# A token-mixing and channel-mixing layer over eight sequences: the low-rank products in other PSUM banks, the chunk products copied by two engines, and a new order of the steps

## The reference, cut to what matters

```python
xn  = ln(x);  sx = shift(xn) - xn
xxx = tanh((xn + sx * maa_x) @ maa_w1)          # 5 low-rank parts of 32
x5  = xn + sx * (maa_stack + xxx @ maa_w2)      # 5 mixes of 512
w   = exp(-exp(time_decay + tanh(x5[1] @ decay_w1) @ decay_w2))
r, k, v = x5[3] @ Wr.T, x5[0] @ Wk.T, x5[2] @ Wv.T
g   = silu(x5[4] @ Wg.T)
# per head, token by token:  out = r . (u * k v + s);  s = k v + w * s
x   = x + group_norm(out) * g @ Wo.T
xn2 = ln(x);  xk, xr = mixes of xn2 and its shift
x   = x + sigmoid(xr @ ffn_Wr.T) * (square(relu(xk @ ffn_Wk.T)) @ ffn_Wv.T)
```

## Time and profile before

| | us |
|---|---|
| median of 3 timed runs (lowest, highest) | 770.8 (770.7, 773.09) |
| the profiled execution, its own time | 774.99 |
| its span | 773.2 |
| TensorE busy in the span | 699.0 |
| VectorE busy | 526.0 |
| GpSimd busy | 391.6 |
| ScalarE busy | 326.6 |

### The profile page before, as it was taken

How to read it: one execution, slowest core, us unless ns; L and a number is a source line. 1 busy time by engine, 2 the same in 40 slices (tenths; PEclk the granted TensorE clock), 3 DMA queues, 4 the chain that set the end, 5 groups by cost and what they waited for, 6 DMA issues and landing times.

```text
span 773.2 us, 17240 instructions
## 1 busy us (share of the span) xinstructions
PE 699.0 (90%) x7260; PEld 478.7 (62%) x7260; DVE 526.0 (68%) x771; ACT 326.6 (42%) x639; POOL 391.6 (51%) x223
## 2 busy tenths in 40 slices
PE   2798889998999899998899989998999979995777
PEld 2586576657774676656675676755876557753453
DVE  3628846896768847796668965886767944679541
ACT  1053463328531583328441394316642274324311
POOL 1054953556566565566356665557456634463000
PEclk9999599999999999999999999999999979999689
DMA  6900000002000200002000020002000010000000
GB/s 205 392 2 8 29 2 1 1 2 89 3 1 1 86 7 1 3 1 90 3 1 1 18 73 2 0 2 90 3 1 1 5 59 3 27 2 1 3 27 27
DMA packets 13130, 24.57 MB, mean 32 GB/s; under 512 B 3840, under 2 KB 5632, under 8 KB 12032
## 3 DMA queue, kind: packets, MB, share of 16 engines
q1 hardware_dynamic: 13056, 23.47, 8.8%
HBM read 18.35 MB, written 4.19 MB: 29 GB/s over the span
## 4 chain that ended last, share of the span: by engine, by line
PE 82%; DVE 7%; issue 5%; ACT 4%; SPq 1%; DMA 1%; POOL 0%; POOLq 0%; ACTq 0%; DVEq 0%
PE FB L588 28%; PE FA L874 8%; PE BAB L856 7%; PE FB L596 7%; PE FA L897 6%; PE BAB L762 5%; PE FA L667 4%; PE BAB L833 3%; PE BAB L799 2%; PE FB L632 2%; PE BAB L579 2%; ACT wide L1040 2%; PE BAB L813 1%; DVE half L1377 1%; PE FB L628 1%
## 5 line engine op out<-in xcount | busy, mean ns | idle before, releaser
L503 POOL TENSOR_TENSOR pp<-rT,kT 128x2048 f32<-128x2048 f32 (+1 forms) x32 | 108.9, 3413 | 58.5 <-DVE rT L1281 58.5
L465 POOL TENSOR_TENSOR mixes<-mixes 128x1024 f32<-128x1024 f32 x30 | 76.6, 2552 | 116.1 <-ACT mixes L1010 116.1
L467 POOL TENSOR_TENSOR mixes<-mixes,xnT 128x1024 f32<-128x1024 f32 x30 | 74.4, 2478 | 2.4
L588 PE MATMUL FB<-mixes,wk_s 128*128 128x256 f32 x256 | 63.0, 400 | 0.1
L874 PE MATMUL FA<-wide,fk_s 128*128 128x256 f32 x256 | 59.7, 394 | 2.3 <-DVE wide L1541 2.2
L1377 DVE TENSOR_REDUCE half<-half 128x256 f32<-128x2048 f32 (+2 forms) x30 | 61.0, 2033 | 0.3
L588 PE MATMUL FB<-mixes,wv_s 128*128 128x256 f32 x256 | 60.6, 386 | 0.0
L588 PE MATMUL FB<-mixes,wg_s 128*128 128x256 f32 x256 | 59.9, 386 | 0.0
L897 PE MATMUL FA<-fv_s,wide 128*128 128x512 f32 x128 | 59.0, 606 | 0.0
L588 PE MATMUL FB<-mixes,wr_s 128*128 128x256 f32 x256 | 58.6, 380 | 0.0
L596 PE MATMUL FB<-fr_s,wide 128*128 128x512 f32 x128 | 58.4, 599 | 0.0
(11 more groups left out here) (168 smaller groups left out, 1343.5 us busy)
## 6 DMA issues: line engine op xcount, KB each, us to landing
pp<-x SPq DMA_DIRECT2D x8, 512.0 KB, 4.4
xt<-x SPq DMA_DIRECT2D x8, 512.0 KB, 3.7
out<-wide SPq DMA_DIRECT2D x7, 512.0 KB, 2.9
half<-wv SPq DMA_DIRECT2D x1, 1024.0 KB, 5.0
wk_s<-wk SPq DMA_DIRECT2D x1, 1024.0 KB, 7.3
wr_s<-wr SPq DMA_DIRECT2D x1, 1024.0 KB, 8.6
wg_s<-wg SPq DMA_DIRECT2D x1, 1024.0 KB, 10.6
wo_s<-wo SPq DMA_DIRECT2D x1, 1024.0 KB, 12.6
```

The lines of the kernel that those rows point to most:

```text
L465: nc.gpsimd.tensor_tensor(slot, slot, sx, ALU.mult).then_inc(s_["mixm_ready"], 1)
L467: nc.gpsimd.tensor_tensor(slot, slot, xnT[:, :, 1:L + 1], ALU.add).then_inc(s_["mix_ready"], 1)
L503: ins = nc.gpsimd.tensor_tensor(pp[:, i % 2, 0:size].rearrange("p (n i j) -> p n i j", i=m, j=m), spread(r.unsqueeze(3), 3, m), spread(k.u ...
L588: ins = nc.tensor.matmul(dst[:, c * L:(c + 1) * L], weight[:, q, c * P:(c + 1) * P], src[:, q, :], start=(q == 0), stop=(q == C - 1))
```

## The change

1. **Banks.** From the third sequence on, the low-rank products go to BB and no longer to FB. They wait for q4_ready of the sequence in the back (its mul4) and no longer for the gate; f_dec1 and f_dec2 now wait for gate0 and gate1, since they write FB. b_ktok waits for both tanh, since it writes BB.
2. **Chunk products.** In every window with a back, ScalarE copies only the half of the chunk products that lies in BA (two instructions for each of kv0 and kv1), VectorE the half in BB (`b_kvx0`, `b_kvx1`, two instructions each). `kvhalf_ready` goes.
3. **Order.** All lists get a new order; no step is added but b_kvx0 and b_kvx1 in second, main and end. In main, b_g3 and b_ktok now stand between f_m20 and f_m21; in first, VectorE does f_xin ahead of f_centre.

```diff
     tensor=dict(
         first="""
-            f_norm warm6 f_lora1 f_pair1 f_lora0 f_m20 f_k0 f_k2 f_k3 f_k1 f_dec1 f_dec2 f_pair3 f_v0 f_v1
-            f_v2 f_v3 f_r0 n_turn f_r2 f_r1 f_r3 f_vtok""".split(),
+            f_norm warm6 f_lora1 f_pair1 f_lora0 f_m20 f_k0 f_k2 f_k1 f_pair3 f_dec1 f_v0 f_k3 f_v1 f_v2
+            f_v3 n_turn f_dec2 f_r0 f_r2 f_r1 f_r3 f_vtok""".split(),
         second="""
-            b_g0 f_lora0 b_g1 b_score0 f_lora1 b_score1 f_m20 b_g2 b_g3 f_dec1 b_score2 b_score3 f_m21
-            b_score4 f_dec2 f_m22 b_ktok b_kv0 b_kv1 f_k0 f_m23 f_k1 b_acc f_k2 f_v0 f_v1 b_vtok b_apply0
-            b_apply1 f_k3 b_apply2 b_apply3 f_v2 f_r0 f_v3 b_gn0 b_gn1 f_m24 b_wo0 b_wo1 f_r1 b_norm20 f_r2
-            b_norm21 f_r3""".split(),
+            b_vtok b_g0 f_lora0 b_g2 f_lora1 b_score0 f_m20 b_g1 b_g3 b_score1 b_score2 f_m21 f_dec1
+            b_score3 f_dec2 b_score4 f_m22 f_m23 b_ktok b_kv0 b_kv1 f_k0 f_k1 f_k2 f_v0 b_acc f_v1 b_apply0
+            b_apply1 f_m24 b_apply2 b_apply3 f_k3 f_r0 f_v2 f_v3 b_gn0 b_gn1 b_wo0 b_wo1 f_r2 b_norm20
+            b_norm21 f_r1 f_r3""".split(),
         main="""
-            c_fk b_score0 c_fr0 c_fv0 b_score1 b_g0 b_score2 f_norm c_fr1 b_score3 b_g2 b_g1 b_g3 b_score4
-            c_fv1 b_ktok f_lora0 f_lora1 b_vtok f_m20 f_m21 b_kv0 f_dec1 b_kv1 f_dec2 b_acc f_m22 f_k0 f_k1
+            c_fk b_score0 c_fr0 b_score1 c_fv0 b_g0 b_score2 c_fr1 b_score3 f_norm b_g2 b_g1 b_score4 c_fv1
+            f_lora0 f_lora1 b_vtok f_m20 b_g3 b_ktok f_m21 b_kv0 f_dec1 b_kv1 f_dec2 f_m22 b_acc f_k0 f_k1
             f_k2 b_apply0 b_apply1 f_k3 b_apply2 b_apply3 f_v0 f_v1 f_m23 f_v2 b_gn0 b_gn1 f_m24 f_v3 b_wo0
             b_wo1 f_r0 f_r1 b_norm20 b_norm21 f_r2 f_r3""".split(),
         end="""
-            c_fk c_fr0 b_score0 c_fr1 b_score1 b_g0 b_score2 f_norm b_g1 b_g2 b_score3 b_g3 c_fv0 c_fv1
-            f_lora0 b_score4 f_m20 f_lora1 b_vtok f_dec1 f_m21 b_ktok b_kv0 b_kv1 f_dec2 b_acc f_m22 f_k0
-            f_k1 f_m23 b_apply0 b_apply1 f_k2 b_apply2 f_k3 b_apply3 f_v0 f_v1 f_m24 f_r0 b_gn0 b_gn1 f_r1
-            b_wo0 b_wo1 f_v2 f_v3 b_norm20 b_norm21 f_r2 f_r3""".split(),
+            c_fk b_score0 f_norm c_fr0 b_score1 b_g0 b_g1 c_fv0 b_score2 c_fr1 b_score3 c_fv1 b_score4 b_g2
+            b_g3 f_lora0 f_lora1 b_vtok f_m20 f_m21 b_ktok f_dec1 b_kv0 b_kv1 f_dec2 f_m22 b_acc f_k0 f_k2
+            f_m23 f_k1 b_apply0 b_apply1 f_k3 b_apply2 f_v0 b_apply3 f_v1 f_m24 f_v2 f_v3 b_gn0 b_gn1 f_r0
+            b_wo0 b_wo1 f_r2 f_r1 b_norm20 b_norm21 f_r3""".split(),
         last="""
-            c_fk b_score0 c_fr0 b_score1 c_fr1 b_score2 b_g0 b_g1 b_g2 b_score3 b_g3 b_score4 b_vtok c_fv0
+            c_fk b_score0 c_fr0 b_score1 b_g0 c_fr1 b_score2 b_g1 b_g2 b_score3 b_g3 b_score4 b_vtok c_fv0
...
     vector=dict(
         first="""
-            f_centre f_xin f_mix1 f_mix2 f_mix0 n_stats f_centre0 n_norm n_xin""".split(),
+            f_xin f_centre f_mix1 f_mix2 f_mix0 n_stats n_norm f_centre0 n_xin""".split(),
         second="""
-            b_prodx b_step1 b_mul0 b_step2 b_mul1 b_gate0 f_mix0 b_step4 b_red1 b_mul2 b_gate1 b_red2 b_mul3
-            b_step8 b_mul4 b_red3 b_red4 b_kv b_scan n_stats b_exp b_var0 b_var1 b_root b_nrm0 b_nrm1 b_gn
-            b_wo0 b_wo1 b_xhat20 b_xhat21 n_norm b_norm2 b_xr""".split(),
+            b_prodx b_step1 b_step2 b_mul0 f_mix0 b_mul1 b_step4 b_gate0 b_red1 b_mul2 b_gate1 b_red2 b_mul3
+            b_red3 b_step8 b_mul4 b_red4 b_kvx0 b_kvx1 n_stats b_kv b_scan b_exp b_var0 b_var1 b_root b_nrm0
+            b_nrm1 n_norm b_gn b_wo0 b_wo1 b_xhat20 b_xhat21 b_norm2 b_xr""".split(),
         main="""
-            b_step1 b_mul0 b_step2 c_mul0 b_mul1 b_step4 b_red1 b_mul2 b_red2 b_mul3 b_step8 b_red3 b_mul4
-            b_gate0 b_gate1 f_xin c_mul1 b_red4 f_mix0 b_kv b_scan b_exp b_var1 b_var0 b_root b_nrm0 b_nrm1
-            n_stats b_gn b_wo0 b_wo1 b_xhat20 b_xhat21 b_norm2 b_xr n_norm""".split(),
+            b_step1 b_mul0 b_step2 b_mul1 b_red1 b_step4 c_mul0 b_mul2 b_red2 b_mul3 b_red3 b_mul4 f_xin
+            c_mul1 b_step8 b_red4 f_mix0 b_gate0 n_stats b_gate1 b_kvx0 b_kvx1 b_kv b_scan b_exp b_var1
+            b_var0 b_root b_nrm0 b_nrm1 b_gn b_wo0 b_wo1 b_xhat20 b_xhat21 n_norm b_norm2 b_xr""".split(),
         end="""
-            b_step1 b_step2 b_mul0 b_mul1 b_step4 b_red1 b_mul2 b_red2 b_mul3 b_gate1 b_gate0 b_red3 b_step8
-            f_xin c_mul0 c_mul1 b_mul4 f_mix0 b_red4 b_kv b_scan b_exp b_var0 b_var1 b_root b_nrm0 b_nrm1
+            b_step1 b_mul0 b_step2 b_mul1 b_step4 b_gate0 b_red1 b_mul2 b_red2 b_mul3 b_red3 f_xin b_mul4
+            b_step8 c_mul0 c_mul1 b_red4 f_mix0 b_gate1 b_kvx0 b_kvx1 b_kv b_scan b_exp b_var0 b_var1 b_root
...
         last="""
-            b_prodx b_step1 b_mul0 b_step2 b_mul1 b_red1 b_step4 b_mul2 b_red2 b_gate0 b_mul3 b_gate1 b_red3
-            b_mul4 b_step8 c_mul0 b_ktok b_red4 b_kvx0 b_kvx1 b_kv b_scan b_exp b_var1 b_var0 b_root b_nrm0
-            b_nrm1 b_gn c_mul1 b_wo0 b_wo1 b_xhat20 b_xhat21 b_norm2 b_xr""".split()),
+            b_prodx b_step1 b_mul0 b_step2 b_mul1 b_step4 b_red1 b_mul2 b_gate0 b_red2 b_mul3 b_gate1 b_red3
+            b_mul4 b_step8 b_red4 b_ktok b_kvx0 b_kvx1 b_kv b_scan b_exp b_var0 b_var1 b_root b_nrm0 b_nrm1
+            b_gn c_mul0 c_mul1 b_wo0 b_wo1 b_xhat20 b_xhat21 b_norm2 b_xr""".split()),
...
     scalar=dict(
...
         main="""
-            c_fk0 c_fk1 c_fr0 c_fr1 b_g0 f_norm b_decays b_g1 f_lora0 b_rcopy b_ktok f_lora1 b_vtok f_mix1
-            b_kv0 f_dec1 b_kv1 f_dec2 f_mix2 b_exp f_k0 f_k1 b_sq1 b_sq0 f_mix3 b_gn f_v0 f_v1 f_mix4
+            c_fk0 c_fk1 c_fr0 c_fr1 f_norm b_rcopy f_lora0 b_g0 f_lora1 b_vtok b_ktok f_mix1 b_decays b_g1
+            f_dec1 b_kv1 b_kv0 f_dec2 f_mix2 b_exp f_k0 f_k1 b_sq0 b_sq1 f_mix3 b_gn f_v0 f_v1 f_mix4
+            b_norm2 f_r1 f_r0""".split(),
...
+        def lora_bank(b):
+            return FB if first(b) else FA if second(b) else BB
...
                 def run(b, par, n):
-                    bank = FA if second(b) else FB
+                    bank = lora_bank(b)
...
                     if not first(b) and not second(b):
-                        pe.wait_ge(s_["g_ready"], 2 * b - 1 + i)
+                        pe.wait_ge(s_["q4_ready"], b)
...
             def f_dec1(b, par, n):
                 loaded("dw", 16 * 3)
                 pe.wait_ge(s_["th_ready"], 2 * b + 2)
+                if not first(b):
+                    pe.wait_ge(s_["g_ready"], 2 * b - 1)
...
             def f_dec2(b, par, n):
                 pe.wait_ge(s_["dech_ready"], b + 1)
+                if not first(b):
+                    pe.wait_ge(s_["g_ready"], 2 * b)
...
             def b_ktok(b, par, n):
                 pe.wait_ge(s_["keys_ready"], b + 1)
                 pe.wait_ge(s_["q4_ready"], b + 1)
+                if not first(b) and not last(b):
+                    pe.wait_ge(s_["th_ready"], 2 * b + 4)
...
-                    for r in range(1 if last(b) else RG):
-                        at = t * (NC // T) + r * PER + 1
-                        k = min(PER, NC - at)
-                        bank = (BA, BB)[r]
...
+                    at = t * (NC // T) + 1
+                    for dst, off in ((kvs[:, :, :, :], 0), (kvodd, S)):
+                        ins = nc.scalar.activation(dst[:, :, :, at:at + PER].rearrange("p d c n -> p c n d"),
+                                                   chunk_states(BA, t, PER, off), ACT.Copy,
+                                                   scale=pm_s[:, off // S:off // S + 1])
+                    ins.then_inc(s_["kvfree_ready"], 1)
...
                 def run(b, par, n):
                     dve.wait_ge(s_["kv_ready"], T * b + t + 1)
+                    if t == 0 and not last(b):
+                        dve.wait_ge(s_["xhatT_ready"], 2 * b + 4)
+                    if t == 0 and not first(b):
+                        dve.wait_ge(s_["expa_ready"], 2 * b)
...
             def b_kv(b, par, n):
 
-                if last(b):
-                    dve.wait_ge(s_["kvfree_ready"], T * b + T)
-                    dve.wait_ge(kvx_ready, T)
-                else:
-                    dve.wait_ge(s_["kvhalf_ready"], T * b + T)
+                dve.wait_ge(s_["kvfree_ready"], T * b + T)
+                dve.wait_ge(kvx_ready, T * b + T)
```

41 lines of the change are left out of this document (16 added, 25 removed).

## The result

The changed kernel has a median of 748.4 us over 4 runs (745.47 to 749.5), the kernel before 770.75 beside it; the ratio is 0.970 [0.966, 0.973]. It is faster, and lies inside the range of 731 to 757, 7.4 us above the 741 forecast. It is outside the forecast's own band of 731 to 745 (0.50) and inside that of the clock rival, 745 to 752 (0.22). The profiled execution took 749.5 us with a span of 747.7.

The account below looks back on a forecast made before the run. TensorE was taken to bound the kernel (82% of the chain), so only its idle time and slow-clock stretches could be won. Terms -10 - 2 - 9 - 5 - 4 = -30 gave 745 profiled, 741 us timed; range 731 to 757.

Parts of the forecast that it names:

- clock rival: Half clock falls elsewhere as waits are cut up and moved; each main window keeps a stretch: 748, band 745 to 752, 0.22.
- Start, -10: First window: f_xin ahead of f_centre on VectorE brings f_k0 from 33.27 to 23.6; -10 us, -7 if a weight is late.
- Window second, -2: Window second: no fewer waits but better fillers, -5 at full clock, less some 3 for half clock; -2, ends -6 and +3.
- Main windows, waits, -9: Five main windows: f_m21's wait for f_mix0 goes and ScalarE's copy chain shortens; 1.8 us a window, -9, ends 0.8 and 2.4.
- Main windows, clock, -5: Half-clock stretches behind f_m21's wait in three of five main windows, 1.7 us each, all go; -5, other end 0.
- GpSimd blocks the copies (3 in 100): Rival: VectorE's four new copies slow fourfold beside GpSimd's mixes, 6.7 us a window in seven windows, +47, 788 us; chance 0.03.
- End window, -4: End window: VectorE's four kv copies bring f_k0 from c_fk + 56.3 to c_fk + 52.5; -4, ends -6 and -1.
- Last, 0: Last window and end, on VectorE's chain: earlier b_step4 gains 1.2 us, score2 comes 1.5 later; 0, ends -1.5 and +1.5.
- The conversion: Whole kernel: 745 in the profiled execution's terms becomes 741, as the timed median was 4.2 us below the profiled 774.99.

Follow-up runs that it names:

- e1: The kernel before with one edit: in VectorE's list of the first window f_xin stands ahead of f_centre; 765.1 us, ratio 0.991.
- e0: The changed kernel run again unaltered, beside three later runs on the same chip; 748.8 us, ratio 0.974.
- e8: The changed kernel with b_gate1 ahead of n_stats on VectorE (main) and GpSimd's f_mix2 made to wait for scan_ready; 750.0 us, ratio 0.975.
- e2: The kernel before with only the copy split: VectorE copies the BB half of the chunk products in second, main and end; 763.9 us, ratio 0.990.
- e6: The changed kernel with all four engines' lists of the window second as before, b_kvx0 and b_kvx1 put into VectorE's; 744.4 us, ratio 0.965.
- e3: The changed kernel with b_g3 moved back ahead of b_score4 in TensorE's main list; 760.7 us, ratio 0.985.
- e7: The changed kernel with b_ktok between f_m20 and f_m21 in TensorE's list of the end window; 747.9 us, ratio 0.974.
- e11: The changed kernel with old lists in second, f_centre's subtractions behind f_mix1 at the start, b_ktok ahead of f_m21 in end; 742.9 us, ratio 0.962.
- e9: The changed kernel with n_stats of the main windows moved behind b_exp on VectorE, so b_gate1 follows b_gate0; 755.1 us, ratio 0.982.

## Why the forecast came out right, and where it was off

- **Start, -10.** Right in mechanism and place (e1: 8.3 to the first c_fk). f_k0 was read right (23.6, is 23.85). The term was 1.5 too large in this profile, and what it lacks is the clock, not the wait for L1250, which was in the layout. With half clock for 3.4 us the first b_g0 is 8.5 us earlier than before, with 6.8 us of it 7.0 (e0), and with none 10.1, at the same wait of 2.74 us (e8). The kernel before has no half clock there; that the new wait brings it is likely (nine of the ten profiles with this wait have it) and not shown, as e2, which has the start of the kernel before, is at half clock from 16.9 to 27.1.
- **Window second, -2.** The step that failed; measured +0.7. The layout named the waits rightly (score2, score3, score4, f_m23, b_ktok), and three of the five came within 0.7 us of their size (score3 was read as 2.4 and is 0.67, score4 2.8 and 1.79). What was wrong is the claim that better fillers make up for them. The idle time of this window went from 9.8 to 12.3 us. By e6 these lists cost 3.1 us of window, while the rest of the change won 2.4 in it (77.78 before, 75.33 in e6). That gain is the copies': with them alone the window takes 75.28 (e2).
- **Main windows, waits, -9.** Measured -6.7. The wait for f_mix0 is gone, b_g3 and b_ktok cover it, and the low-rank products start without a wait. Each window gained 1.3 instead of 1.8 in the mean, and 2.0 of the 6.7 us are luck: they are the loss late in b_apply of the third window, which the prediction had said would stay. There VectorE's pair now starts ahead of GpSimd's product (5.82 us, before 7.60), an order that nothing in the prediction counted on. The other four windows gained 0.8 each in this profile, 1.1 in e0's. I first put the difference down to f_dec2's wait for the gate, 0.9 to 1.5 us where I had read 0.5. That theory fell with e8: without the wait the idle time is no smaller. What it is in place of that is shown for two windows of five (the pause inside L842); for the other three it stays open.
- **Main windows, clock, -5.** Measured -6.8. The three stretches behind f_m21's wait are gone, as forecast (5.1 us); the fourth, 1.7 us, is again the third window's, behind the pause that was to stay. It hangs on little: with b_g3 in its old place stretches return in three windows (e3), and with the main lists unchanged one stands in the profile of e7 and one in that of e11.
- **GpSimd blocks the copies (3 in 100).** False: 0.50 to 0.69 us each. The Trainium skill (SBUF — State Buffer, Who interferes with whom) also says that VectorE does contend when both of its inputs are in SBUF and GpSimd reads SBUF, and that issue order decides who is blocked. The trace agrees for L1428, whose inputs kvs and cm_s are both SBUF tiles: 5.8 us first, 7.5 second. I had used the rule for the new copies only, and had not looked for where it would bite: the pair next to them, with 0.13 us between the two starts in the window shown.
- **End window, -4.** Measured -4.0, and f_m21 directly behind f_m20 waits 1.76 us as read (1.8); f_k0 is at c_fk + 52.1 (read as 52.5). But the match is in part luck. Of the 4.0 us, 2.0 are idle time and 2.0 the clock, and that part changes between executions of one order. Against the 91.49 us of e1, which has the old order there, the gain is 1.4 us, or 1.2 with e0's 90.29.
- **Last, 0.** Measured -0.1.
- **The rival of the clock gave 748**, and that is the time found, but not for its reason: the main windows keep no half clock in either profile of the changed kernel. The first c_fk, forecast near 125, is at 129.56, by the first two terms.
- **The conversion.** I took the 4.2 us by which the profiled execution of before stood above its median as lasting. After the change that distance is 1.1. So of the 7.6 us between 740.8 (770.8 - 30) and 748.4, 4.5 are the terms (30 against 25.5) and 3.1 this.

## What to carry to other kernels

When two engines that can block one another come free at about the same time, read which one starts first and by how much; a margin of 0.1 us and less decides over microseconds, and an edit that makes everything a little earlier can turn it. Before a gain in one stage is booked to an edit, look at that stage in a second profile of the same order: here the clock alone moved an end window by 2.6 us. A wait that the trace shows on the bounding engine is not yet a gain: take it out and see whether the idle sum falls. And a wait cut into several small ones can cost more than the one it came from, so price a new order by the sum of its waits.

## What the runs showed of the hardware that I had not expected

- VectorE's product of two SBUF tiles and GpSimd's product hold each other up in order of their start: first by 0.01 to 0.11 us is enough (e9, e11). The pair takes 5.8 to 5.9 or 7.5 to 7.75 us, its first product 1.9 or 3.8 to 4.05, GpSimd's product 2.4 if just ahead and 3.4 to 4.1 if behind.
- TensorE can stop for 0.8 to 2.4 us in the middle of a run of small matmuls with no semaphore between them: behind 48 of 64 in the first and third main window of the changed kernel, of e0 and of e8. Instructions are loaded by a queue of their own in that stretch (q8 in the view of transfers, three packets from 180 to 192 us in the changed kernel); that the pause is a wait for them is argued, not shown. Where f_dec2's wait ahead of it was shortened by 0.9 us, the pause was 2.08 in place of 0.96 us (e8, first window).
- Stretches at half clock differ between two executions of one kernel: from 22.7 to 26.1 and from 599.6 to 603.0 in one profile of the changed kernel, from 22.3 to 29.2 and from 599.2 to 606.0 in the other (e0), which is half of TensorE's busy time in them, 3.4 us, more at the same median.
